# First unit of a conditional LoRA MLP by plain block products, and the loads and boundary units around it in another order

## What is computed

```python
x = x + einsum('bct,bcd->bdt', x, L0_weights[cond])
x = x + einsum('bct,bcd->bdt', x, L1_weights[subj])
x = x + einsum('bct,bcd->bdt', x, L2_weights[subj]) + bias[subj][:, :, None]
gate = lora_linear(x, Wg, Ag, Bg, subj)      # x@W + (x@A[subj])@B[subj]
up   = lora_linear(x, Wu, Au, Bu, subj)
h    = silu(gate) * up
x    = x + lora_linear(h, Wd, Ad, Bd, subj)
```

## Time and profile before

| | us |
|---|---|
| median of 3 runs (lowest, highest) | 1323.35 (1322.71, 1323.93) |
| profiled run, its own time | 1325.06 |
| span of the profile | 1323.3 |
| TensorE busy | 1291.5 (98%) |
| VectorE busy | 1012.0 (76%) |
| ScalarE busy | 544.7 (41%) |
| GpSimd busy | 566.2 (43%) |

### The profile page before, as it was taken

One profiled execution on the slowest core, in us unless ns is written; L12 is line 12 of the kernel. 1 busy time (PEld: TensorE's weight loads), 2 busy tenths in 40 slices (PEclk: granted clock), 3 DMA queues, 4 the chain that ended last, 5 costly groups with the idle time before them and its releaser, 6 DMA issues.

```text
span 1323.3 us, 17419 instructions
## 1 busy us (share of the span) xinstructions
PE 1291.5 (98%) x6118; PEld 1067.7 (81%) x6118; DVE 1012.0 (76%) x1525; ACT 544.7 (41%) x940; POOL 566.2 (43%) x468
## 2 busy tenths in 40 slices
PE   7899999999999999999998999999999999999998
PEld 6677888888878888888887888888887888888886
DVE  5886778777777777778768777787877877777775
ACT  2643444444344444544324434444442434433331
POOL 2255456435405455445421554554431443334440
PEclk7999999999999999999999999999999999999999
DMA  4546245344726334445273524444445522223321
GB/s 149 165 147 199 88 148 156 121 144 125 289 82 207 100 108 148 121 146 156 89 296 116 171 94 126 136 143 137 130 178 189 177 82 74 92 89 100 100 64 64
DMA packets 100565, 180.19 MB, mean 136 GB/s; under 512 B 9344, under 2 KB 53632, under 8 KB 100480
## 3 DMA queue, kind: packets, MB, share of 16 engines
q1 hardware_dynamic: 83040, 124.96, 29.5%
q0 software_dynamic: 17152, 54.02, 12.4%
q10 hardware_dynamic: 288, 0.10, 0.0%
HBM read 143.92 MB, written 35.13 MB: 135 GB/s over the span
## 4 chain that ended last, share of the span: by engine, by line
PE 89%; DVE 5%; DMA 2%; POOL 2%; issue 1%; ACT 1%; ACTq 0%; SPq 0%; DVEq 0%
PE px L1227 26%; PE pd L1227 26%; PE py L1227 13%; PE pv L1227 7%; PE pz L1227 6%; PE pz L1244 3%; PE pd L1455 1%; PE px L1244 1%; PE py L1244 1%; DMA w_raw<-w_gu 1%; DVE acc L1091 1%; PE pd L1254 1%; PE pd L1317 1%; DVE wg_lo L935 1%; DVE u L1118 1%
## 5 line engine op out<-in xcount | busy, mean ns | idle before, releaser
L554 POOL TENSOR_TENSOR h_lo<-g,h_hi 128x512 fp32r<-128x512 f32 x128 | 176.8, 1381 | 401.2 <-ACT h_hi L627 400.0
L536 POOL DMA_INDIRECT b_got<-b_table,idx_b x192 | 193.9, 1010 | 263.3 <-PE py L1244 197.9
L1067 DVE TENSOR_TENSOR acc<-pd,acc 128x512 f32<-128x512 f32 x256 | 174.0, 690 | 69.9 <-PE pd L1227 65.8
L1227 PE MATMUL px<-xo_hi,wg_hi 128*128 128x512 f32 x544 | 218.8, 402 | 4.2 <-ACT g L818 1.5
L627 ACT ACTIVATE wg_hi<-w_raw 128x512 fp32r<-128x512 f32 (+1 forms) x272 | 155.6, 574 | 155.6 <-PE py L1244 84.2
L1227 PE MATMUL px<-xo_hi,wg_lo 128*128 128x512 f32 x544 | 214.6, 394 | 0.0
L1227 PE MATMUL px<-xo_lo,wg_hi 128*128 128x512 f32 x544 | 212.8, 391 | 0.0
L935 DVE TENSOR_TENSOR wg_lo<-w_raw,wg_hi 128x512 fp32r<-128x512 f32 (+1 forms) x272 | 192.1, 709 | 18.3 <-ACT wg_hi L627 17.0
L1227 PE MATMUL pd<-wd_hi,h_hi 128*128 128x512 f32 x512 | 201.7, 394 | 1.7 <-POOL h_lo L554 1.7
L1227 PE MATMUL pd<-wd_hi,h_lo 128*128 128x512 f32 x512 | 199.9, 390 | 0.0
L1227 PE MATMUL pd<-wd_lo,h_hi 128*128 128x512 f32 x512 | 199.1, 389 | 0.0
(11 more groups left out here) (230 smaller groups left out, 2282.1 us busy)
## 6 DMA issues: line engine op xcount, KB each, us to landing
w_raw<-w_gu SPq DMA_DIRECT2D x68, 512.0 KB
wd_raw<-w_dn SPq DMA_DIRECT2D x64, 320.0 KB
xo_hi<-xops SPq DMA_DIRECT2D x21, 512.0 KB, 5.9
xo_lo<-xops SPq DMA_DIRECT2D x21, 512.0 KB, 7.0
acc<-x SPq DMA_DIRECT2D x8, 1024.0 KB, 7.5
out<-acc SPq DMA_DIRECT2D x7, 1024.0 KB, 6.0
xops<-st_hi SPq DMA_DIRECT2D x24, 256.0 KB, 2.8
xops<-st_lo SPq DMA_DIRECT2D x24, 256.0 KB, 2.9
```

The source lines that it names most:

```text
L536: gp.indirect_dma_start(out=dst, out_offset=None, in_=rows_of, in_offset=bass.IndirectOffsetOnAxis(ap=rows.bitcast(U32), axis=0)).then_inc ...
L554: return gp.tensor_tensor(dst, src_raw, src_hi, ALU.subtract)
L1067: ins = dve.tensor_tensor(dst, pd[j][:, :], dst, ALU.add)
L1227: ins = pe.matmul(psum, w_parts[wi], x_parts[xi], start=(start and i == 0), stop=(stop and i == 2), skip_group_check=more)
```

## The change

Unit 0 is made by eight plain block products instead of seven with sums, 48 matmuls for 42. Each of its four results stays in a PSUM bank of its own (`first_banks`), and `ua_high` and `ua_low` read it there; `sums(0)`, `c11(0)`, `u3(0)`, `c12(0)` and the keeping copies of unit 0 are gone. The block A21 is split as an operand of its own, and the token sums S1 to S4 are first used by unit 1. Two groups of matmuls without a result between the products (`warm_up`) are gone. The loads of the opening wait for other events, `b_low(0)` moves from DVE to POOL, and an index computation (`block_rows`) moves to the start of DVE's list. Unit 1 ends with two of its `lora` products, and boundary units have an order of their own on ACT and DVE. In odd units POOL makes `h_low(q, b, 0)` before all six gathers. Counts of the semaphores go from n + 1 to n, since unit 0 no longer adds to them.

```diff
+        first_banks = ((px, py), (pz, pv))
...
+            return (py, pz, pv) if q and not t else (pd[0], pd[1], pd[2])
...
+            return (((0, 0), (1, 1), (0, 1), (1, 0)) if q else ((0, 0), (0, 1), (1, 0), (1, 1))).index((t, m)) + 1
...
-            sp.wait_ge(pick_made, TP)
+            sp.wait_ge(pick_made, TP + 2)
             load_weights(0)
+            sp.wait_ge(oe_in[0], TP * 16)
             load_x(0, 1)
             load_b(0)
...
+            b_low(0)
...
-                if gathers:
-                    gp.wait_ge(b_out[max(0, m - 1)], piece_out(max(0, m - 1)))
-                    gp.wait_ge(p3_mm, n + 1)
-                    gather_b(to_q, m, 0, range(0, 2))
                 h_low(q, b, 0)
                 j = parts_at(q, b)
                 if j is not None:
                     gp.wait_ge(turn_hi, 2 * turns(q, j))
                     low(part(st_lo[:, 4:7, :]), st_lo[:, 4:7, :], st_hi_of(4)).then_inc(turn_lo_p, 1)
                 if gathers:
-                    gather_b(to_q, m, 0, range(2, CHUNKS))
+                    gp.wait_ge(b_out[max(0, m - 1)], piece_out(max(0, m - 1)))
+                    gp.wait_ge(p3_mm, n)
+                    gather_b(to_q, m, 0)
...
+                    gp.wait_ge(p4_mm, n)
                     gather_b(to_q, m, 1)
...
-            for g in (0, 2, 1, 3):
-                weights_high(0, g)
-            b_high(0)
...
+                if t == 0:
+                    b_high(0)
...
-                if q:
+                if not q:
+                    src = first_banks[t][m]
+                    act.wait_ge(first_mm, 2 * t + m + 1)
...
+            act.wait_ge(o_a2_kept, TP)
+            copy(xo_hi[:, A22, :], a2_raw[1]).then_inc(o_hi, 1)
+            copy(wd_hi[:, :, 0:TOK], a2_raw[0].rearrange("p (c n) -> p c n", c=2)).then_inc(o_hi, 1)
+            ua_high(0, 0, 0)
             sum_high(S1, o_s1_sum)
-            keep_s1(0)
-            copy(xo_hi[:, A22, :], a2_raw[1]).then_inc(o_hi, 1)
             sum_high(S2, o_s2_sum)
-            keep_s5(0)
+            ua_high(0, 0, 1)
             sum_high(S3, o_s3_sum)
-            keep_s2(0)
             sum_high(S4, o_s4_sum)
-            ua_high(0, 0, 0)
+            act.wait_ge(first_mm, 3)
             weights_high(1, 0)
-            act.wait_ge(p2_mm, 1)
             weights_high(1, 1)
+            ua_high(0, 1, 0)
+            b_high(1)
             ua_high(0, 1, 1)
-            ua_high(0, 0, 1)
-            b_high(1)
             weights_high(1, 2)
...
                     weights_high(n + 1, 0)
                 if b:
                     act.wait_ge(h_done[0], blocks_done(q, b - 1))
                 keep_s2(n)
-                if not last and b <= 1:
+                if b == -1:
+                    ua_high(q, 0, 0)
+                    ua_high(q, 1, 1)
+                    ua_high(q, 0, 1)
+                    act.wait_ge(p4_mm, n)
+                    act.wait_ge(h_lo_done[1], blocks_done(q, -1))
+                    copy(g1[:, :], px[:, :]).then_inc(c21_kept, 1)
+                    ua_high(q, 1, 0)
...
+                        weights_high(n + 1, g)
+                    v_high(q - 1, 1)
+                    weights_high(n + 1, 3)
+                    continue
...
+                if (q, b) == (0, 0):
+                    keep_c21()
...
+            block_rows()
...
-            sums(0)
+            for g in range(4):
+                dve.wait_ge(w_hi_done[g], 1)
+                dve.tensor_tensor(wg_lo[:, 2 * g, :], w_raw[:, 0, g, :], wg_hi[:, 2 * g, :], ALU.subtract
+                                  ).then_inc(w_done[g], 1)
             picked(1)
...
+            selectors(0, 0)
             sums(1)
...
-            o_low(S1, s_raw[S1])
+            o_low(A22, a2_raw[1])
+            dve.wait_ge(o_hi, HIGH_ORDER.index(A21) + 1)
+            for c in range(2):
+                ins = dve.tensor_tensor(a21(1, c), a2_raw[0][:, c * TOK:(c + 1) * TOK], a21(0, c), ALU.subtract)
+            ins.then_inc(o_done, 1)
...
+                if b == -1:
+                    v_low(q - 1, 0)
+                    c11(n)
+                    u3(n)
+                    ua_low(q, 0, 0)
+                    c12(n)
+                    ua_low(q, 1, 1)
+                    ua_low(q, 0, 1)
+                    sums(n + 1)
+                    weights_low(n + 1, 0)
+                    ua_low(q, 1, 0)
+                    weights_low(n + 1, 1)
+                    select(q, 0)
+                    weights_low(n + 1, 2)
+                    finish(q - 1, 0)
+                    weights_low(n + 1, 3)
+                    selectors(q, 1)
+                    continue
+                if b == 0:
+                    if q:
+                        v_low(q - 1, 1)
+                    c11(n)
+                    u3(n)
+                    if not q:
+                        sums(n + 1)
+                    select(q, 1)
+                    if not q:
+                        weights_low(n + 1, 0)
+                        weights_low(n + 1, 1)
+                    c12(n)
+                    gate0()
+                    if q:
+                        sums(n + 1)
+                        weights_low(n + 1, 0)
+                    c22()
+                    if q:
+                        weights_low(n + 1, 1)
+                    gate1()
+                    weights_low(n + 1, 2)
+                    weights_low(n + 1, 3)
+                    if q:
+                        finish(q - 1, 1)
+                    continue
...
+                            ins = pe.matmul(select_bank(q, t, m, c), sel[:, part, c * P:(c + 1) * P], ua[:, t, m, tokens],
                                             start=(part == 0), stop=(part == 1))
                 ins.then_inc(sel_mm, 1)
...
+            def first_product(t, m):
+                halves = ((A11, A12), (A22, A21))[t]
+                for i, k in enumerate(halves):
+                    g = ((0, 1), (3, 2))[m][i if t == 0 else 1 - i]
+                    pe.wait_ge(w_done[g], 1)
+                    if t:
+                        pe.wait_ge(o_done, LOW_ORDER.index(k) + 1)
+                    for c in range(2):
+                        ws, xs = slice(c * P, (c + 1) * P), slice(c * TOK, (c + 1) * TOK)
+                        xs = [a21(0, c), a21(1, c)] if k == A21 else [xo_hi[:, k, xs], xo_lo[:, k, xs]]
+                        ins = split_product(first_banks[t][m][:, :], [w[:, 2 * g, ws] for w in (wg_hi, wg_lo)], xs,
+                                            start=(i == 0 and c == 0), stop=(i == 1 and c == 1))
+                ins.then_inc(first_mm, 1)
+            pe.wait_ge(o_a1_done, 1)
+            pe.wait_ge(o_a2_kept, 1)
+            first_product(0, 0)
+            pe.wait_ge(o_a2_kept, 2)
+            first_product(0, 1)
+            pe.wait_ge(o_a2_kept, TP)
+            first_product(1, 0)
+            first_product(1, 1)
...
                 ins = product(px, A22, False, True)
                 if not adapters:
...
                 ins.then_inc(p4_mm, 1)
+                if n == 1:
+                    lora(py, b, 1, 0).then_inc(p3_mm, 1)
+                    lora22()
```

430 lines of the change are left out of this document (202 added, 228 removed).

## The result

The changed kernel takes 1310.94 us in the median of 4 runs (1307.75 to 1312.72) against 1323.05 before (1322.71 to 1323.93): a ratio of 0.9905, interval 0.9885 to 0.9925. It is faster by about 12 us; 24 had been forecast, and the time lies just above the stated range. The same kernel timed once more gave 1309.08 (ratio 0.9889, interval 0.9872 to 0.9907). The first profiled execution took 1311.19 us, the second 1309.55.

What follows compares the result with a forecast made beforehand. PE, busy 1291.5 of 1323.3 us, was taken as the bound, with gains in idle time and low clock. From 1325.06, -9.7 (opening) and -14.5 (boundaries) gave 1300.9 profiled, median 1299; range 1292 to 1310.

Steps and rivals of the forecast that it cites:

- The chain that ends the opening is DVE's: Opening: DVE, busy nearly throughout up to unit 1's last weights, sets the pace; its chain gets 1.5 us shorter.
- Loads, clock, second wait: Opening: gather wait of 4.25 us gone, full clock worth 5.1 us, new 1.5 us wait; DVE's low parts start at 26.4.
- Unit 2's load: End of opening: load delayed 1.7 us on SP and 0.4 in the queues; sums start at 57.4, 7.2 us ahead.
- The chain behind it: Behind unit 2's load: chain to the last low part shrinks from 9.6 to about 9.0 us; unit 2 fed 7.8 ahead.
- the clock behind PE's idle stretch: End of unit 1: up to 5 us idle lowers PE's clock beside DVE's chain, counted as 0.3 us.
- POOL's order: First units: making h_lo ahead of the gathers removes the waits of two `pd` products, -1.7 us.
- The boundaries: Three quarter boundaries: waits for low parts (-5.6 us) and `u` (-3.9) go, lower clock (-5.1) too; -14.5 in all.
- rival D: Boundaries: one kind of wait moves to the weights' first group or `lora22`; +5 to +9 us, 1306; chance 0.10.
- B: Opening: the clock stays low over transposes and small matmuls, costing 3.6 to 5 us, about 1303; chance 0.14.
- C: Opening: transfers do not hinder each other, no second-gather wait or unit 2 load delay; 3.6 us less, 1295; chance 0.10.
- E: Opening: gathers land no earlier, so the 4.25 us wait and the clock stay; +9 us, 1308; chance 0.04.
- F: Odd units: first gathers behind h_lo come too late for PE, making the kernel slower, 1330 and more; chance 0.04.

Runs made afterwards that it cites:

- e15: The changed kernel timed and profiled once more, unchanged: 1309.08 us.
- e9: Changed kernel with unit 2's weights first on SP, unit 1's selection first on DVE, POOL's low part of the B table's second piece later: 1302.59 us.
- e4: Changed kernel with unit 2's weights load issued on SP ahead of the down weights, the B table's load and its two stores: 1306.75 us.
- e14: Kernel before with one wait added on SP, so the down weights load behind unit 1's last low part: 1326.83 us, ratio 1.0030.
- e1: Changed kernel with the ACT and DVE lists of boundary units (b = -1 and 0, quarters 1 to 3) as before: 1321.82 us.
- e3: Changed kernel with the opening's loads as before (weights behind four picks, x's second half and B table at once): 1316.86 us.
- e5: Changed kernel with DVE's selection of unit 1 ahead of the sums of unit 2's weights: 1309.06 us.
- e6: Changed kernel with 32 identity matmuls without a result while PE waits for `u` in unit 1: 1310.56 us.
- e7: Changed kernel with 12 identity matmuls ahead of the first half's matrices in the opening: 1311.40 us.
- e10: Changed kernel with boundary units, POOL's gathers in odd units and the opening's loads all as before: 1329.84 us, ratio 1.0059 to the kernel before.
- e13: First unit alone plus unit 2's weights first on SP, selection first on DVE, POOL's B-table low part later: 1322.12 us, ratio 0.9989 to the kernel before.

## Why the prediction was wrong

The step that failed is the opening's: "The chain that ends the opening is DVE's" with the paragraph on unit 2's weights behind it, in all -9.7 us. It brought -3.9 in the second profile and -2.3 in the first. In its place the runs show 1.6 us more in DVE's chain, 1.4 in the load, 1.9 in the chain behind it, and 1.6 of lower clock in unit 2. The second profile (e15), whose execution lacks the late signal, can be read step by step.

- **Loads, clock, second wait.** Forecast: no wait for the gathers, full clock, a new wait of 1.5 us, low parts on DVE at 26.4. Measured: no wait, the clock 1.00 to 22 us, a wait of 1.7 us before the second combination, 26.63. Right, in each term. In the first profile a signal of PE came 2.5 us late, PE idled 1.7 us, and the clock fell to 0.67 in the window behind it: that execution started the low parts at 28.37. Behind an idle stretch the Trainium skill (TensorE: Matmul & The Clock Gate, Part 1: The HAM clock gate) expects the half rate. This window agrees; the second profile's idle stretch of the same 1.7 us was followed by 1.00.
- **DVE's chain** to unit 1's last low part: forecast 24.8 us, measured 26.4 (26.63 to 53.0). By its start times this chain takes 26.3 us in both kernels (34.21 to 60.47, 26.63 to 52.97), where 1.5 less was forecast. About half of the difference is stretched instructions. The selectors' 1.71 us for 0.95 and one low part's 1.79 for 0.69 make 1.86 us, and in both POOL was making a low part at the time; e9 shows it for the second. But the old chain held such a stretch too, which I had not seen, so 0.8 us remain of it:

```profile
55.70 2.39 DVE L935 TENSOR_TENSOR wg_lo<-w_raw,wg_hi 128x512 fp32r<-128x512 f32 x2
```

Two low parts take 1.29 us alone, and POOL's `st_lo` stands at 55.32 to 56.94. The other half is idle time that was not there to be won. I took 1.7 us of 2.3 as gone, but 0.9 of the 2.3 lie ahead of 34.21; the waits inside the chain were 1.3 us before (0.38, 0.55, 0.39), and 0.45 are left.

- **Unit 2's load.** Forecast 6.2 us from the last low part to the sums, with a delay of 2.1 in it; measured 7.6 (53.0 to 60.60). The mechanism was right (e4, and e14 in the kernel before), the size too small, mainly in the queues: from issue to the first sum the load takes 5.5 us for the 4.4 forecast. The reason lies in the order of the low parts: S4's moved to just before the last weights, and `load_down` waits for it, so it meets the weights' load; before, it was 9 us ahead.
- **The chain behind it** was put at 9.0 us, and takes 10.95 (60.60 to the next load at 71.55). The two last low parts, 3.21 us in place of 1.1, stand beside POOL's h_low, and two low parts at 63.60 take 1.83 for 1.28 beside its `st_lo`. That is 2.7 us of stretching, for 1.0 in the same chain before (72.15, 1.72 for 0.69). No experiment moved these, so here the cause is argued from the rows and from e9.
- **Where it ends.** The last three miss by 1.6 + 1.4 + 1.9 = 4.9 us, and of the 7.8 us by which unit 2's split was to be ahead, 2.75 are left at the next load (71.55 for 74.30). For the clock behind PE's idle stretch I had counted 0.3 us. The window of 0.64 looks like a loss of 2.8, but DVE's unbroken row beside it shows that it did not hold up the next load.
- **A clock term that I had not counted.** Behind two short waits in unit 2 (1.1 us for g, 1.2 for u3) the clock falls again: 0.56 from 80 to 82 us and 0.59 from 82 to 84 in the second profile. From the load for unit 4 to the one for unit 5 it then takes 18.8 us (85.11 to 103.88; 86.78 to 105.52 in the first profile), where e1, e3, e4, e5, e6 and e9, at 1.00 there, take 17.2 and the kernel before 17.1. That is 1.6 us on the path, in both profiles of the changed kernel.
- **POOL's order** was forecast at -1.7 and measured at -1.95, within the noise.
- **The boundaries** were forecast at -14.5. At the boundaries themselves it is -14.8, waits and clock as forecast. I had written that the weight sums "then press on b = 1" and set no price to it: 3 x 1.07 us come back there. That is like a small form of rival D, but with the old lists (e1) PE waits for u3 too, so how much of it is the sums' new place stays open. e1 puts the lists' whole worth at -10.9 by the medians and at -13.0 by the two profiles' rows.
- **The sum.** -9.7 and -14.5 were forecast; the first profile gave -2.3 and -11.6, the second -3.9 and -11.6 (its end is 15.5 us ahead).
- **The rivals.** B, the opening's clock, is not it: in the second profile the clock is 1.00 in the first half's layers, and the opening still misses by 5.8 us. In the first profile a low clock there does cost some of the 1.7 us. e7 could not price it. C named the right place and the wrong sign: the transfers were more in each other's way, not less. E and F are out. None of them held the possibility that the first unit by itself is a loss; e10 shows that it is. e13 shows that three places in the new lists of SP, DVE and POOL make up that loss within the noise, so that none is left for the plain products themselves.

What stays open is why PE's signal came 2.5 us late in some executions (see the last section), what share of the difference between the medians 1310.94 and 1309.08 it has, why the clock in unit 2 falls in some profiles and not in others, and what loses 1.4 us in the three later quarters.

## What to carry to other kernels

When the work of one engine's chain is put in another order, follow the load that the chain's end releases: what else waits for the same event and stands ahead of it in the DMA issuer's list costs twice, on the issuer and in the queues. One line of issue order was worth 2 to 4 us here. Count each engine's instructions with what the neighbour does at the same time, in the old list as well as in the new one, and when sums are moved behind something, price what then comes late in the next unit.
